# Pooling steps, their exponentials and one block product put in another order in a two-layer kernel

## The reference, cut to what matters

```
h = gelu(x @ fc1_w.T + fc1_b)                     # hidden size 2048, exact gelu
x = x + concat(h @ fc2_w.T + fc2_b,               # 384 shared outputs
               h @ experts_w[idx[b]].T + experts_b[idx[b]])   # 128 outputs of the batch's expert
s = tanh(x @ W1 + b1) @ v                         # one score a token, W1 is 512 x 128
p = softmax(where(mask, s, -1e30))                # mask by type: l <= j, l >= j, or l != j
x = x + (p @ x) / count(mask)
```

## Time and profile before

| | us |
|---|---|
| median of 3 runs (1350.90 to 1351.01) | 1350.99 |
| the profiled execution | 1351.38 |
| its span | 1349.6 |
| PE busy | 1302.4 (97%) |
| DVE busy | 1075.9 (80%) |
| ACT busy | 966.7 (72%) |
| POOL busy | 261.8 (19%) |

### The profile page before, as it was taken

One profiled execution on the slowest core, in us unless ns is written; L12 is line 12 of the kernel. 1 busy time (PEld: TensorE's weight loads), 2 busy tenths in 40 slices (PEclk: granted clock), 3 DMA queues, 4 the chain that ended last, 5 costly groups with the idle time before them and its releaser, 6 DMA issues.

```text
span 1349.6 us, 25573 instructions
## 1 busy us (share of the span) xinstructions
PE 1302.4 (97%) x9849; PEld 960.2 (71%) x9849; DVE 1075.9 (80%) x2092; ACT 966.7 (72%) x1764; POOL 261.8 (19%) x380
## 2 busy tenths in 40 slices
PE   9999999999999999999999999999999999999998
PEld 4458476577867778677786877868678686777856
DVE  7988898668869687796877868688596886968798
ACT  5768868586786867768577685877868678686772
POOL 0000101022212122222122211222112321222202
PEclk9999999999999999999999999999999999999999
DMA  8540223136344363534536254363543634436206
GB/s 293 163 111 18 63 75 83 40 90 122 87 116 93 104 135 71 122 77 119 115 86 126 64 133 95 94 126 71 125 92 95 121 86 112 93 103 125 66 15 121
DMA packets 73884, 136.43 MB, mean 101 GB/s; under 512 B 9746, under 2 KB 34210, under 8 KB 71330
## 3 DMA queue, kind: packets, MB, share of 16 engines
q0 software_dynamic: 28032, 56.63, 24.4%
q1 hardware_dynamic: 45154, 77.38, 17.2%
q10 hardware_dynamic: 576, 0.79, 0.2%
HBM read 45.65 MB, written 18.87 MB: 48 GB/s over the span
## 4 chain that ended last, share of the span: by engine, by line
PE 78%; DVE 11%; ACT 5%; DMA 3%; issue 2%; SPq 0%; POOL 0%; DVEq 0%; ACTq 0%; POOLq 0%
PE ps L547 13%; PE ps L549 13%; PE ps L548 13%; PE ps L649 12%; PE ps L660 5%; PE ps L657 4%; PE ps L636 3%; PE ps L637 3%; PE ps L638 3%; DMA hl<-hl 2%; ACT L1199 1%; DVE hl L1731 1%; DVE hh L1731 1%; ACT space L1202 1%; ACT g L1034 1%
## 5 line engine op out<-in xcount | busy, mean ns | idle before, releaser
L547 PE MATMUL ps<-xh,w1h 128*128 128x256 f16 x960 | 261.8, 273 | 1.5
L548 PE MATMUL ps<-xl,w1h 128*128 128x256 f16 x960 | 261.7, 273 | 0.0
L549 PE MATMUL ps<-xh,w1l 128*128 128x256 f16 x960 | 261.7, 273 | 0.0
L1034 ACT ACTIVATE g<-ps,b1s,ds 128x512 f32<-128x512 f32 x240 | 173.4, 773 | 65.4 <-PE ps L549 65.4
L547 PE MATMUL ps<-xh,ch 128*128 128x256 f16 x720 | 196.3, 273 | 1.5
L549 PE MATMUL ps<-xh,cl 128*128 128x256 f16 x720 | 196.2, 273 | 0.0
L548 PE MATMUL ps<-xl,ch 128*128 128x256 f16 x720 | 196.2, 273 | 0.0
L1619 DVE SCALAR_TENSOR_TENSOR hl<-g,ix,hh 128x512 f16<-128x512 f32 x243 | 175.9, 745 | 3.1
L1008 ACT ACTIVATE hh<-g,ix 128x512 f16<-128x512 f32 x243 | 161.6, 718 | 0.0
L649 PE MATMUL ps<-hh,w 128*128 128x512 f16 x576 | 134.1, 379 | 0.0
L2657 POOL DMA_DIRECT2D g<-space x30 | 36.9, 1230 | 487.9 <-DMA g<-space 444.5
(11 more groups left out here) (364 smaller groups left out, 3080.4 us busy)
## 6 DMA issues: line engine op xcount, KB each, us to landing
space<-in_xT SPq DMA_DIRECT2D x62, 256.0 KB, 3.2
g<-space SPq DMA_DIRECT2D x60, 256.0 KB, 2.6
er<-in_ew SPq DMA_DIRECT2D x15, 1024.0 KB, 4.8
out<-space SPq DMA_DIRECT2D x60, 256.0 KB, 3.2
space<-space POOLq DMA_DIRECT2D x52, 256.0 KB, 3.3
hl<-hl POOLq DMA_DIRECT2D x24, 512.0 KB, 7.9
g<-space POOLq DMA_DIRECT2D x30, 256.0 KB, 3.9
g<-g POOLq DMA_DIRECT2D x30, 256.0 KB, 4.0
```

Source lines behind the costliest of these rows:

```text
L547: mm(to, wh, mh, start=i in (1, 5) and c == 0, stop=False, skip_group_check=True)
L548: mm(to, wh, ml, start=False, stop=False, skip_group_check=True)
L549: m = mm(to, wl, mh, start=False, stop=c == 1, skip_group_check=True)
L1034: act(in_two(g_of(b, k)), src, ACT.Gelu, bias=b1s[:, k:k + 1], scale=ds1[:, b % 2, p:p + 1]).then_inc(gelu_done)
```

## The change

- PE: in a batch behind a paired one, product5 of pair 2 goes ahead of product1. sum1 E no longer waits for the evacuation of the second chunk; ACT's `first_of_sum` waits for it instead. In the opening of batches 0 to 2 `score` goes ahead of product3.
- ACT: in a paired batch `one_way_exponentials(b - 1)` goes from behind `first_of_sum` E to behind the last expert split, ahead of `e_squares`. `inverses` goes to where the exponentials were, and the second of two x splits ahead of `second_of_sum` S.
- DVE: batch 3 does 22 pooling steps ahead of its paired part in place of 17, and the batches after it 18; the paired part has 2, 4, 6, 2 and 2. `late` has a new place, behind `add_second` of the last pair and ahead of the expert's low parts. `bounds` goes behind `third_sum`.
- POOL: the first part of `mend` becomes `fetch`, which stands behind `third_low_sum`.

```diff
         def cycle(b, c):
...
+            elif paired(b - 1):
+                product5(b, c)
+                product1(b, c)
             else:
                 product1(b, c)
             if c < PAIRS:
-                product5(b, c)
+                if c > 2 or not paired(b - 1):
+                    product5(b, c)
...
             if v == EXPERT:
-                e.wait_ge(x2_done, nth_chunk(b, 1))
                 e.wait_ge(el_done, nth_chunk(b, 3))
...
             product4(n, 0)
+            score(b)
             product3(n, 0)
-            score(b)
...
             e.wait_ge(s_done, nth_product(b, v, 1))
+            if v == EXPERT:
+                e.wait_ge(x2_done, nth_chunk(b, 1))
...
             split_expert_high(b, 3)
             if b == LAST:
                 break
+            if paired(b):
+                one_way_exponentials(b - 1)
             e_squares(b + 1)
...
                 first_of_sum(b, EXPERT)
-                one_way_exponentials(b - 1)
+                inverses(b - 1)
                 split_x_high(b + 1, X11)
+                split_x_high(b + 1, X21)
                 second_of_sum(b, STATIC)
-                split_x_high(b + 1, X21)
...
                 third_of_sum(b, STATIC)
-                inverses(b - 1)
...
-            takes = ((0, 3, 1), (1, 1, 1), (1, 2, 1), (1, 1, 1), (1, 1, 1), (0, 0, 0))
-            late = (0, 0, 0)
+            takes = ((0, 1, 1), (1, 1, 1), (1, 1, 1), (1, 1, 1), (1, 1, 1), (0, 1, 1))
+            late = (1, 0, 1, 0)
...
+            elif b == 3:
+                takes = ((0, 3, 1), (1, 1, 1), (1, 2, 1), (1, 1, 1), (1, 1, 1), (1, 1, 1))
...
             add_second(b, PAIRS - 1)
+            pool(late[2])
...
             expert_low(b, 0)
             expert_low(b, 1)
-            pool(late[2])
+            pool(late[3])
...
                 expert_sum2(b)
                 pool(2)
+                third_sum(b)
                 bounds(b + 1)
-                third_sum(b)
-                pool(3)
+                pool(4)
                 second_sum(b, hh)
                 second_sum(b, hl)
                 batch_scales(b + 1)
                 expert_sum3(b)
                 add_left(b, STATIC)
                 add_left(b, EXPERT)
-                pool(7)
+                pool(6)
                 first_sum(b, hh)
...
                 add_second(b + 1, 0)
-                pool(3)
+                pool(2)
...
+            if b > 2:
+                fetch(b - 2)
             e.wait_ge(*combined_by(b, T3))
```

More of the change, by code:

```diff
@@ L2265, in vector_program @@
         for b in range(1, B):
-            takes = ((0, 3, 1), (1, 1, 1), (1, 2, 1), (1, 1, 1), (1, 1, 1), (0, 0, 0))
-            late = (0, 0, 0)
+            takes = ((0, 1, 1), (1, 1, 1), (1, 1, 1), (1, 1, 1), (1, 1, 1), (0, 1, 1))
+            late = (1, 0, 1, 0)
             if b == 1:
-                takes, late = ((0, 0, 0),) * 5 + ((1, 1, 1),), (2, 2, 2)
+                takes, late = ((0, 0, 0),) * 5 + ((1, 1, 1),), (2, 2, 0, 2)
             elif b == 2:
-                takes, late = ((0, 3, 1), (1, 1, 1), (1, 2, 1), (1, 2, 0), (1, 2, 0), (2, 2, 0)), (1, 1, 3)
+                takes, late = ((0, 3, 1), (1, 1, 1), (1, 2, 1), (1, 2, 0), (1, 2, 0), (2, 2, 0)), (1, 1, 0, 3)
+            elif b == 3:
+                takes = ((0, 3, 1), (1, 1, 1), (1, 2, 1), (1, 1, 1), (1, 1, 1), (1, 1, 1))
             elif b == LAST:
-                takes, late = ((0, 3, 1), (1, 1, 1), (1, 2, 1), (0, 0, 0), (0, 0, 0), (1, 0, 0)), (1, 1, 2)
+                takes, late = ((0, 1, 1), (1, 1, 1), (1, 1, 1), (0, 0, 0), (0, 0, 0), (1, 0, 0)), (1, 1, 0, 1)
             for c, (one, two, three) in zip(range(2, PAIRS), takes):
@@ L2608, in add_other, with fetch @@
             eng.dma_start(out[b, :, c, 0:S - 1], pooled_rows(b, c)[1][:, 1:S], accum_op=ALU.add).then_inc(second_added, 16)
[L2610 to L2615, removed]
+        tokens_at = {}
+        def fetch(n):
+            done, is_c, lone, held = pool_value(n, 0), e2[:, n:n + 1], cell(n, 19), cell(n, 34, 4)
             e.wait_ge(pool_step, done + 2)
@@ L2619, in mend @@
                 e.wait_ge(s_step, s_value(n, ALL_ADDED))
-            at = eng.value_load(cell(n, 8)[0:1, :].bitcast(i32), min_val=0, max_val=S - 1)
+            at = tokens_at[n] = eng.value_load(cell(n, 8)[0:1, :].bitcast(i32), min_val=0, max_val=S - 1)
             eng.tensor_copy(held, flat(xr[:, n % XB, :, bass.ds(at, 1)])).then_inc(mend_step)
@@ L2624, in mend @@
             eng.tensor_scalar(held, held, lone, is_c, ALU.mult, ALU.mult).then_inc(mend_step)
+        def mend(n):
+            at = tokens_at[n]
+            done, is_c = pool_value(n, 0), e2[:, n:n + 1]
+            inverse = cell(n, 23, 2)
+            share, rest, both, one = cell(n, 38), cell(n, 39), cell(n, 40, 4), cell(n, 44, 4)
             e.wait_ge(pool_step, done + 16)
```

## The result

| | median us | range, runs | ratio to before, 95% interval |
|---|---|---|---|
| before | 1350.95 | 1350.90 to 1351.01, 4 | |
| changed | 1431.07 | 1430.15 to 1434.29, 4 | 1.0597 [1.0579, 1.0616] |

The change costs 80.1 us. The forecast was 1416 us, its own range 1408 to 1428, and 1380 to 1430 with the first rival. The profiled execution took 1430.15 us, span 1428.4, mean granted clock 0.974; before it was 1351.38, 1349.6 and 1.0.

What follows compares the result with a forecast made beforehand. PE, busy 97%, bounds the kernel with its waits on DVE sums behind ACT's exponentials. sum5 comes 5.4 us late in each of 12 batches, 65 us on 1351.4, so 1416 us; range 1408 to 1428, or 1380 to 1430 with the first rival.

Steps and rivals of the forecast that it cites:

- the first rival: At sum6 the move is not late and only DVE's list counts: 34 us more, 1385 us; chance 0.25.
- Which step stands at the new place, and DVE's stall: On DVE, step 11, which waits for ACT's exponentials, lands ahead of the expert's low parts; DVE stands still some 10 us.
- sum1 waits 2.5 us: PE at sum1 needs tile 15's low part, done at 724.71 and not 718.33, so it waits some 2.5 us.
- sum6's `hl` half waits for the move: PE's `hl` half of sum6 waits through DVE's sum for the late `hl<-hl` move and goes 5.05 us late.
- I take the distance as fixed: On POOL the move still goes out 8.71 us after tile 12's low part starts, with T3 and T1 ahead of it.
- The clock: PE's granted clock was read as full in every slice before the change; the forecast has no term for it.
- The third rival: Moves beside later puts, or the fourth sums, delay sum3 E or T4 as well: 1430 to 1440 us; chance 0.06.
- Product5 first: PE, pair 2, product5 ahead of product1: bounds 0.58 us a batch gained, 0.3 lost; taken as 0.
- Table load without a drain: ACT's table load to DVE's step 11 takes 2.57 us, with no drain of 1.38 us; with one, about 1433 us.
- The move by its row: The `hl<-hl` move lands 6.3 us after issue in the median, by the trace, not 3.2 us by the skill's rule.
- The faster rival: If DVE step 11 started by 714.7, PE would save up to 20 us at sum6: 1331 us; chance 0.05.

Runs made afterwards that it cites:

- the fillers: Changed kernel with matmuls without use in PE's two long waits, 24 ahead of sum1 and 26 ahead of sum6's second half: 1428.3 us, ratio 1.0575.

## Why the prediction was wrong, point by point

- *Which step stands at the new place, and DVE's stall*: right. "Some 10 us" was 10.39. The low parts were done 6.0 us after step 11 began, as worked out (756.25 - 750.27 = 5.98, forecast 0.68 + 5.32). Moving this one step took away the whole loss.
- *sum1 waits 2.5 us*: right; 2.59 in the row, 31.8 us in all.
- *sum6's `hl` half waits for the move*: right in kind, and the first rival (1385) is out. The wait was forecast near 3 us; it was 2.86 in the batch shown but up to 4.4, 44.3 in all.
- *The step that failed* is "I take the distance as fixed", from T3 to the move. It was 4.99 us in the earlier trace rows. In the changed kernel it grew from 5.55 in the first paired batch to 7.26 in the last, 6.38 in the mean of the twelve. The move itself landed after 6.1 us in the mean, in place of 6.3. Together, from T3 to the `hl` sum the forecast had 735.8 - (720.72 + 3.72) = 11.36 us, and the mean of the twelve is 12.51: 1.15 us a batch, 13.8 us.
- *That closes the sum.* The profiled executions are 1430.15 - 1351.38 = 78.8 us apart, and 65 + 13.8 is the same, closer than the terms are known. The rest to the 80.1 between the medians is scatter between executions (1430.15 to 1434.29).
- *Why T3 was slower*: two things stood beside it. The first is the puts. The prediction's own working ran the four pairs of low parts in one piece of 5.32 us (they had taken 6.44), and each put follows one of them, but it gave the puts' new places no term. The trace of before had a warning: in its first paired batch the third put went out 0.3 us behind T3 in place of 0.8, and T3 and the move were 6.02 us apart (304.97 to 310.99). Holding two puts shows their part, 4.91 to 4.19 us from T3 to T1 in the fifth paired batch. The second is told below this list.
- *The clock* was read as full in the earlier trace rows, and no term was put for what longer waits of PE do to it. It fell to its lower level in the changed kernel. The traces put its cost at about 0.5 us. The slow sets took up waits that PE would have had: those ahead of sum6 are 9.2 us in all with the fillers and 1.5 without. It is not free everywhere: with step 11 one place later, three slow sets in a row stand behind sum6's wait in six batches, and there the first sum for sum5 comes 10.3 to 10.5 us behind the `hl` sum in place of 9.8.
- The third rival named this side (moves beside later puts, 1430 to 1440) but with 0.06 and with other victims, sum3 E and T4. The measured 1431 lies in its range, though the delay came through T3 and the `hl` sum; PE's sum3 E shows no wait of its own in the changed kernel.
- *Product5 first* costs nothing, right; the gap was 0.62 in place of 0.58 us.
- *Table load without a drain*: right by the row, 2.57 us to step 11 in both kernels. The Trainium skill, "ScalarE: Activation LUTs", section "What ACT_TABLE_LOAD costs", adds a drain of 1.38 us, and the trace of the changed kernel shows none either.
- *The move by its row*: right in size, 5.9 us in the median. The Trainium skill, "DMA: Bandwidth & Descriptors", section "Anatomy of one DMA — SWDGE (gpsimd) path", has a fit that gives an estimate of 3.2 us for 512 KB, and the trace does not agree here either.
- *The faster rival* was priced at 1331 if step 11 stood behind the low parts. There it does reach 1327.5, so the price was right. Its low chance was for the change as it stood, and its condition did not hold there.

T3's distance to the move is 5.6 to 5.9 us in the first six paired batches and 6.8 to 7.3 in the last six, with the puts at the same places. The traces point at a second neighbour. (The DMA view of the changed kernel from 844.4 to 850.5 us lists one packet of `q8 instruction`, that from 667.8 to 672.3 us none.) In each of the last six a packet of 16 KB of the queue that the profile calls `instruction` starts 2.0 to 4.0 us behind T3; in the first five there is none while T3 is under way, and in the sixth it starts 4.7 us behind. In the kernel with fillers the first, sixth and eleventh batch have it and are the slow ones. Over the changed kernel and those with fillers and with step 11 one place later, T3 landed after 5.7 to 6.2 us in the 15 batches where such a packet starts 2.0 to 4.0 us behind it, and after 4.4 to 5.2 in the other 21. That is a coincidence in time, seen in 36 of 36 batches; no run moves such a packet by itself, so that it slows T3 is likely but not shown.

## What to carry to other kernels

Before an instruction that waits is moved ahead in an engine's list, write down when its releaser ends and all that is queued behind it; one step of 0.7 us cost 103.5 us here by its place alone, with the stall itself on an engine that is busy 75% of the time. An earlier signal pays only if the waiting step stays where that signal is already there. When work bunches together, take no transfer behind it at its old duration: put a term for the transfers that now run side by side.

## What the runs showed of the hardware

- In the changed kernel the granted clock fell behind 20 of the 24 PE waits of 2.59 to 4.38 us (eight 128x256 matmuls then took up to 1.71 us from start to start of the sets in place of 0.87). It did not fall behind the other four (2.60 to 2.86 us), and not in the kernel before, where the longest wait in a paired batch was 1.5 us. With 24 and 26 matmuls without use in those waits the mean was 0.998 in place of 0.974. Yet the fall cost about 0.5 us of 1431, since PE would have waited for others in that time.
- Accumulating transfers inside SBUF and plain puts slow each other: with two puts held, T3 landed 0.6 to 2.0 us sooner, batch by batch, and the move took 7.1 us in place of 5.9. Beside the move, T3 took 6.2 to 7.9 us in place of 4.5 to 6.2.
- POOL's T1 went out 0.35 to 0.37 us after T3 had landed in every paired batch, 4.2 to 6.5 us behind T3, though the kernel has no wait for that landing; the move went out 0.74 us behind T1 while T1 was under way. With the move ahead of both, T3 went out 0.62 us behind the move and T1 again only after T3 had landed. What holds T1 is not shown.
